# Two-layer block with experts and state space: ACT's small slots, an earlier sum of outputs, the second experts' table and stores in pieces

## What is computed

```python
h = _layernorm(x) * (1 + ca) + sa
x = x + ga * _L0_attn_ref(h, ...)      # causal attention, 16 heads of 8, rotary
h = _layernorm(x) * (1 + cb) + sb
x = x + gb * _L0_ffn_ref(h, ...)       # 8 experts, top 2 by softmax, a shared expert
h = _layernorm(x) * (1 + ca) + sa      # vectors of the second layer from here on
x = x + ga * _L1_attn_ref(h, ...)      # state space
h = _layernorm(x) * (1 + cb) + sb
x = x + gb * _L1_ffn_ref(h, ...)       # 8 experts of width 352, top 2 by score
```

```python
x_in = x @ in_W.T + in_b
K = jnp.exp(dtA[:, :, None] * jnp.arange(Lseq))
k = 2.0 * jnp.einsum('hn,hnl->hl', Ceff, K).real
y = irfft(rfft(u, n=2 * Lseq) * rfft(k, n=2 * Lseq))[..., :Lseq] + u * D_skip[:, None]
y = gelu(y)
a, g = split(glu_W @ y + glu_b)
out = (a * sigmoid(g)) @ out_W.T + out_b + x
```

## Time and profile before

| what | value |
|---|---|
| three timed runs | 1283.17, 1283.76, 1278.12 us (median 1283.17) |
| profiled execution | 1280.39 us, span 1279.1 us |
| mean granted clock of TensorE | 0.86 of full speed |
| busy share of the span | PE 75%, DVE 66%, ACT 54%, PE's weight loads 49%, POOL 35% |
| front, until its barrier opens | 130.3 us |
| attention, projection, routing and experts of layer 0 | until 865.9 us |
| state space, its gate | until 977.3, until 1010.0 us |
| routing, experts, last sum of layer 1 | to about 1082, 1240, 1279 us |

### The profile page before, as it was taken

The page is one execution under the profiler, slowest core; times in us unless marked ns, Lnnn a source line. Parts: engine busy times, 40 slices in busy tenths (PEclk is TensorE's granted clock), DMA queues, the critical chain, the costliest instruction groups (busy, mean ns, idle before and its releaser), DMA issues. The chain is left out here.

```text
span 1279.1 us, 26922 instructions
## 1 busy us (share of the span) xinstructions
PE 955.5 (75%) x9014; PEld 621.1 (49%) x9014; DVE 848.6 (66%) x2087; ACT 689.3 (54%) x1475; POOL 443.8 (35%) x510
## 2 busy tenths in 40 slices
PE   4554589899998998987477979961756656898990
PEld 2232233333333333324355568861645445898990
DVE  6765788888888888824765336646776786543435
ACT  3684067777777777774334447752602223565660
POOL 5636012322321122210375327760000066674440
PEclk9777589999999999989577989995868855998995
DMA  8125002111111100000211123328553332232216
GB/s 205 66 101 207 29 8 79 42 35 35 50 48 39 35 27 26 2 1 1 64 61 58 38 66 95 96 65 260 136 134 101 101 92 78 70 85 78 64 54 203
DMA packets 116286, 97.16 MB, mean 76 GB/s; under 512 B 15437, under 2 KB 102568, under 8 KB 116152
## 3 DMA queue, kind: packets, MB, share of 16 engines
q1 hardware_dynamic: 101976, 75.30, 20.4%
q0 software_dynamic: 8704, 17.97, 4.1%
q10 hardware_dynamic: 5472, 2.17, 0.6%
HBM read 60.18 MB, written 34.95 MB: 74 GB/s over the span
## 5 line engine op out<-in xcount | busy, mean ns | idle before, releaser
L844 DVE TENSOR_REDUCE part<-sps 128x2 f32<-128x1024 f32 (+2 forms) x320 | 341.6, 1114 | 65.1 <-PE sps L725 43.0
L819 ACT ACTIVATE prob<-tpa 128x1024 f32<-128x1024 f32 (+1 forms) x208 | 193.0, 928 | 77.5 <-PE tpa L761 74.5
L655 POOL TENSOR_SCALAR_AFFINE_SELECT prob<-prob 128x512 f32<-128x512 f32 x128 | 79.7, 634 | 357.0 <-ACT prob L819 357.0
L1578 POOL DMA_INDIRECT yk<-yo,place x144 | 146.8, 1019 | 129.9 <-ACT yo L1607 107.0
L819 ACT ACTIVATE prob<-tpb 128x512 f32<-128x512 f32 (+1 forms) x224 | 128.4, 573 | 63.5 <-PE tpb L761 63.5
L781 PE MATMUL ops<-prob,vs 128*32 128x512 f32 (+3 forms) x1536 | 160.3, 505 | 1.5 <-POOL prob L655 1.5
L718 PE MATMUL sps<-qk 48*128 48x512 bf16 (+3 forms) x768 | 135.6, 344 | 31.7 <-DVE part L844 21.7
L1186 POOL DMA_INDIRECT xg<-h,slot x128 | 124.7, 975 | 84.0 <-DVE slot L1309 46.8
L1691 PE MATMUL banks<-xT,y 128*128 128x128 f32 x864 | 111.3, 280 | 5.1 <-issue 3.5
L1633 DVE COPY place<-xt 128x1 uint32<-128x1 uint32 x144 | 22.0, 153 | 135.9 <-ACT esg L1601 93.4
L1691 PEld LDWEIGHTS banks<-xT,y 128*128 128x128 f32 x864 | 105.4, 197 | 5.6 <-issue 5.6
(11 more groups left out here) (337 smaller groups left out, 1835.1 us busy)
## 6 DMA issues: line engine op xcount, KB each, us to landing
xt<-xg SPq DMA_DIRECT2D x144, 65.0 KB
qk<-term SPq DMA_DIRECT2D x24, 256.0 KB, 2.7
qk<-qk SPq DMA_DIRECT2D x64, 96.0 KB
arena<-kpad SPq DMA_DIRECT2D x6, 1024.0 KB, 11.8
powers<-powr SPq DMA_DIRECT2D x8, 516.0 KB, 5.3
powr<-powers SPq DMA_DIRECT2D x4, 1032.0 KB, 8.8
qk<-qk SPq DMA_DIRECT2D x64, 64.0 KB
arena<-yk SPq DMA_DIRECT2D x16, 256.0 KB, 5.7
```

Source lines behind the costliest of these rows:

```text
L655: nc.gpsimd.affine_select(out=blk, in_=blk, pattern=[[0, HQ], [1, P]], compare_op=ALU.is_ge, fill=0.0, base=0, channel_multiplier=-1).then ...
L819: nc.scalar.activation(prob[:, at:at + len(units), 0:n], slot_of(t, m)[:, :, 0:n], ACT.Exp, scale=float(HD) ** -0.5).then_inc(exp_done, 1)
L844: freed(nc.vector.tensor_reduce(to, src, AX.X, ALU.max, negate=True))
L1578: nc.gpsimd.indirect_dma_start(out=d.yk, out_offset=bass.IndirectOffsetOnAxis(ap=place[:, u:u + 1], axis=0), in_=yo[u][:], in_offset=None) ...
```

## The change

It has three parts, and some small moves that go with them.

**In the front**, ACT's state space work is cut into smaller slots. `scalar(act, s)` becomes `scalar(act, s, place)`: place 0 stands between `high` and `middle`, place 1 at the step's end. The magnitudes spread over steps 2 to 5 and the sines over steps 5 to 8, one group a place (the magnitudes one or two). The kernel sums start in step 7 instead of 5. DVE's coefficients move from its fifth step to its seventh (s == 6). The waits for the landing of the kernels and powers move out of the front into SP's part of the attention; for this the tile `powr` and both semaphores live in the scope around both.

**The first sum** (`first_sum`) begins in the first layer's program. SP issues all 16 gathers of `yk` there, behind the landing of all results, into `w.v` and `w.y`, and DVE does `combine(0)`, `combine(1)` and the first batch's statistics there. In `s4_core` the other parts are summed in another order around the shifts (`AHEAD`, `BEHIND`), and ACT's `norm(b)` also waits for part b + 4. SP loads there the powers first and then the first four kernel matrices without a wait. The output bias is added to `h` in four pieces between copies of states, the passes over h and x at the end are gone, and the residual of the gate phase has three operations: product + h, x gate, + x.

**In the second layer** the sets of weights stand one batch earlier where they can, so that none is left behind the last batch's ranks. The last wave's table is made in four pieces, one a tile at n = 4 to 7. The eight stores of empty rows stand one each behind the loads of tiles 24 to 31, and their landing is waited for ahead of tile 40. The first layer keeps its tables and tails.

```diff
+                    s4.scalar(act, s, 0)
+                    if s > 0:
                         middle(s - 1)
...
-                    s4.scalar(act, s)
+                    s4.scalar(act, s, 1)
...
                     if s == 4:
                         gates()
+                    if s == 6:
                         s4.coefficients(dve)
...
-    SINES = {3: (0, 1), 4: (2, 3), 5: (4, 5), 6: (6, 7)}
-    SUMS = {5: (0, 1), 6: (2, 3), 7: (4, 5), 8: (6, 7)}
+    MAGNITUDES = {(2, 1): (0,), (3, 0): (1, 2), (3, 1): (3,), (4, 0): (4, 5), (4, 1): (6,), (5, 0): (7,)}
+    SINES = {(5, 1): (0,), (6, 0): (1,), (6, 1): (2,), (7, 0): (3,), (7, 1): (4,), (8, 0): (5,), (8, 1): (6, 7)}
+    SUMS = {7: (0, 1, 2), 8: (3, 4, 5, 6, 7)}
+    KERNELS = {(8, 0): (0, 1), (8, 1): (2, 3, 4, 5, 6, 7)}
...
-        sp.wait_ge(p_kept, 16 * NI)
-        sp.wait_ge(k_kept, 16 * (1 + GI))
...
+                    if t == 0:
+
+                        sp.wait_ge(w.k_kept, 16 * (1 + GI))
                     if t < len(rows_of):
...
                 sp.wait_ge(rows_in, 16 * (len(rows_of) - 1))
+                sp.wait_ge(w.p_kept, 16 * (NG // GI))
```

```diff
+                if layer == 0:
+                    sp.wait_ge(experts.sh_added, NB)
+                    for s in range(2 * NB):
+                        w.first.load(sp, s)
+                else:
                     combined.sync(sp)
...
+                if layer == 0:
+                    w.first.combine(dve, 0)
+                    w.first.combine(dve, 1)
+                    w.first.statistics(dve, 0)
+                else:
                     combined.vector(dve)
...
+                AHEAD, BEHIND = ([2], [5], [6], []), ([3, 4], [], [7], [])
                 for b in range(NB):
+                    for s in AHEAD[b]:
+                        combine(dve, s)
+                    shifts(b)
+                    for s in BEHIND[b]:
+                        combine(dve, s)
                     if b + 1 < NB:
-                        combine(2 * b + 2)
-                    shifts(b)
-                    if b + 1 < NB:
-                        combine(2 * b + 3)
-                        statistics(b + 1)
+                        statistics(dve, b + 1)
...
+                    if n % 2 == 1:
+
+                        hb = h[:, n // 2 * TPB:(n // 2 + 1) * TPB, :]
+                        v.tensor_tensor(hb, hb, m.outb[:].rearrange("p (o c) -> p o c", o=1).to_broadcast([P, TPB, C]), ALU.add)
...
                     act.wait_ge(shifted, b + 1)
+                    act.wait_ge(x_done, b + 5)
...
-                    link(v.tensor_tensor(o[u][:], po[:, u, :].rearrange("p (j c) -> p j c", j=4),
-                                         w.gate[:, 2, bass.ds(b, 1), :].to_broadcast([P, 4, C]), ALU.mult))
+                    hs = m.h_keep[:, b * TPB + u * 4:b * TPB + u * 4 + 4, :]
+                    v.tensor_tensor(o[u][:], po[:, u, :].rearrange("p (j c) -> p j c", j=4), hs, ALU.add).then_inc(o_read, 1)
+                    dve.wait_ge(o_read, s + 1)
+                    link(v.tensor_tensor(o[u][:], o[u][:], w.gate[:, 2, bass.ds(b, 1), :].to_broadcast([P, 4, C]), ALU.mult))
```

```diff
+    else:
+        WEIGHTS_AT = [([0, 1], [2]), ([3, 4], [5]), ([6], [7]), ([], [])]
...
-            if layer == 1 and n == 4:
-                routed.tables(dve, len(waves) - 1)
+            if layer == 1 and 4 <= n < 8:
+
+                next(table)
...
             sp.dma_start(xt[n % UN][:], rows[bass.ds(at, 1)][0]).then_inc(x_in[n % UN], 16)
+            if layer == 1 and waves[0][1] <= n < waves[0][1] + NE:
+                routed.tail(sp, n - waves[0][1])
```

136 lines of the change are left out of this document (71 added, 65 removed).

## The result

| | before | changed |
|---|---|---|
| median of four executions each | 1281.82 us | 1249.76 us |
| all four | 1278.12 to 1283.76 | 1245.36 to 1254.02 |
| span of the profiled execution | 1279.1 us | 1244.0 us |

The ratio is 0.9734, with a 95% interval of 0.9704 to 0.9764: 2.7% faster, 32 us. I had forecast 1257 with a range of 1247 to 1268, a gain of 26 against the median then known. The sum was 6 us short of that.

The account below looks back on a forecast made before the run. PE bounds the second experts' stretch; elsewhere whoever reaches the closing barrier last. Terms -6.5, -6.0, +1.1, -3.6, -3.8, -6.6 sum to -25.4, taking 1280.4 to 1255.0 us; forecast 1257 (the profiled execution lay below the median), range 1247 to 1268.

Parts of the forecast that it names:

- Front, -6.5: Front: 2.4 us from the landing, 2 from POOL's chain, 2.1 from SP's queue, together 6.5 us gained.
- the coefficients' 3.8: Front, DVE: the coefficients take 3.8 us and, moved behind the seventh step, end at 91.6, so POOL starts 4.7 later.
- The estimate of 2.9: Front, POOL: by SBUF contention the last four groups cost 2.9 us each, ending the front about 1 us earlier; not summed.
- they run from 119.3 to 123.9: Front, SP: the last four kernel stores, with nothing left ahead of them, start at 119.3 and end at 123.9 us.
- Way into the state space, -6.0: First layer's end: gathers fill SP's idle time, barrier 5.8 us later, first row operation 10.0 behind it, 6.0 gained.
- rival C: Gathers at the first layer's end crowd each other at 1.0 us each: barrier 874.7, gain 2.7, kernel 1260.3; chance 0.07.
- Gate, +1.1: State space gate: a third operation a step costs 1.85 us, fewer semaphores to clear give 0.75 back, 1.1 lost.
- the 14 us of passes: State space's end: removing DVE's three big passes gains nothing, since they ended within 0.1 us of the last store's landing.
- Second layer, -14.0: Second layer's program: earlier weight sets 3.6 us, table in pieces 3.8, stores of empty rows one by one 6.6, all gained.
- All 3.8 go: Second layer's experts: the table in four pieces fits DVE's idle time, removing the whole 3.8 us pause, at the least 3.
- Rival D: Second layer's experts: POOL's scatters replace the removed pauses, the 6.6 us return as waits, kernel 1264; chance 0.08.
- Rival E: Second layer's experts: without the pauses PE gets tiles at half clock, each 2.12 us more, kernel slower or even; chance 0.05.

Follow-up runs that it names:

- c_coef5: Changed kernel with DVE's coefficients one step earlier, on its sixth step (s == 5) instead of the seventh: 1252.27 us, ratio 0.9758 to the kernel before.
- u_slots: Changed kernel with ACT's front slots, coefficients and kernel sums back in their old places, landing still awaited in the attention: 1260.88 us, ratio 0.9838 to the kernel before.
- u_sum: Changed kernel with all 16 gathers, two combinations and first statistics back behind the first layer's barrier, new sum order kept: 1265.77 us, ratio 0.9855 to the kernel before.
- u_gate: Changed kernel with the three output passes back at the state space's end and two gate operations a step: 1365.25 us, against 1370.0 for the changed kernel on the same chip.

## Why the prediction was right, and where it fell short

**Front, -6.5, was -9.3 (-9.8 by the mean of the fronts).** DVE's seventh step ended at 88.4, as forecast (88), but by luck. DVE's waits for the first cast up to there fell by 13.4 (19.9 to 6.5), not by 17; and the coefficients' 3.8, which had stood ahead of this step and now stand behind it, I had not taken off. The two errors cancel. The steps on POOL hold: start at 91.6 forecast, 92.2 measured; end 117.5, measured 117.2; last kernel out of ACT 119.3, measured 119.0. I had priced the last four groups at 3.1, and they took 2.82; the first four took 3.4 each, where I had used 3.65, which is the mean of all eight and not of those beside a busy DVE. The estimate of 2.9 that I had set beside the sum, by the contention that the Trainium skill describes (SBUF — State Buffer, "Who interferes with whom"), was the nearer one. The trace agrees with the page: no pair was above 2.52 once DVE had stopped, each of the two pairs of 3.50 had beside it one DVE operation with two inputs from SBUF (at 99.37 and 103.01), and 3.1 of the 4.5 us by which c_coef5 lengthened the chain fell beside a busy DVE. The term that was mis-sized is "they run from 119.3 to 123.9": the stores took 1.58, not 4.57. I had taken the duration of an issue as its own, though I had just removed what stood ahead of it in the queue. u_slots brought back 4.69 together with the late stores of q and k, and in six profiles the stores' time went roughly with the DMA share just ahead of them. The landing was 2.4, as said.

**Way into the state space, -6.0, was -7.7.** Barrier 5.8 later forecast; 4.8 in this pair of profiles, 4.1 to 5.8 over the others. By the mean of the seven profiles named at u_sum (262.5 and 100.4) the part gives 5.8, so the forecast was closer than the pair shows: the changed kernel's profile in the pair is 1.9 below the mean in these two programs. Sixteen gathers took 12.6, forecast 12.9; rival C (1.0 each) did not happen. From the skill's limit (DMA: Bandwidth & Descriptors, "Where 436 GB/s comes from") they would have taken 11.7; 4.2 MB in 12.6 us are 333 GB/s, and the first eight, 2.1 MB in 5.45, came to 385 GB/s at their issue, above the page's 358. But that is the rate of issue, not of the data: from 844 to 860 the DMA engines, busy all the time (share 1.02), moved 263 GB/s, below the page's limit. The 10.0 from the barrier to the first row operation were exact. Rival C's own number is off by a little: a barrier at 874.7 and 10.0 behind it leave 2.9, not 2.7. What the step didn't see is that SP would hold the barrier by only 1.5 us over DVE.

**Gate, +1.1, was +0.8,** within what the stage varies: 33.0 to 34.2 in the profiles of the changed gate, 32.7 twice in the kernel before. SP's first load comes 2.35 behind the barrier instead of 3.00, near the 0.75 forecast. What the third operation costs stays open: between DVE's first and last operation 1.3 us more than before in this pair, not 1.85, but only 0.2 more than in u_gate, which takes it away again. That the 14 us of passes gain nothing was right: in u_gate they end 2.4 ahead of the barrier.

**Second layer, -14.0, was -13.5,** and the parts were 3.5, 3.0 and 6.3 by the programs' lengths, 3.3, 2.8 and 5.9 by PE's rows, against 3.6, 3.8 and 6.6. The mis-sized term is the table: "All 3.8 go" is not so, since PE's lead over DVE doesn't take the longer pieces. The five tiles from the first piece on lose 0.95, and 3.8 - 0.95 is the 2.8 measured. Rival D did not come: PE waits 0.2 us in the whole stretch, for nothing of POOL's, and is busy 139.76 of 140.00. Rival E was wrong in its direction: without the pauses the clock stayed at full. One number of mine was a slip: "a stretch of the second experts near 144" doesn't follow from my own terms, which give 158 - 10.4 = 147.6. Measured alike it was 9.4 shorter, 148.6. Another slip is the upper end of the range: "with the same spread" D's 1264 reaches 1272, not 1268.

**What was not in the sum** are the attention's 4.4 us and the projection's 1.0, by which the profiled pair differs. They are PE's granted clock in these executions; whether a part of them comes from the change isn't shown. Without them the pair is 29.7 apart; the sum said 25.4, and the 4.3 between are the front's 2.8, the way into the state space with 1.7 and the gate's 0.3, less 0.5 in the second layer. The 1.7 are luck of this pair, as its two programs lie 1.9 below their mean. So by the means of the profiles the touched stages give some 28 of the medians' 32.1, and the last 4 us stay open: the attention varies by 10, and both of its pairs favour the changed kernel by 4.

## What to carry to other kernels

The duration of a DMA's issue in a row belongs to what stands ahead of it in the queue as much as to itself: when an edit empties the queue, reprice the issues behind it (4.6 us became 1.6 here). Where an engine waits at a barrier for another engine's drain, work of the next program that needs only finished data fits there, up to the point where the next engine in line holds the barrier; read all the drains, not only the last. A chain on POOL is shorter beside an idle DVE, so starting it earlier gains less than the head start (7.3 us gave 2.8). And a gain at one operation isn't yet one of the program: the gathers split five and three brought the first row operation 1.2 us forward, and the end of the stage 0.1 to 0.2.

## What the runs showed of the hardware

POOL's drain at the end of a layer's program took 10.5 to 11.4 us in every profile. Its record starts ahead of the last two scatters (854.4, with the last scatter from 856.21 to 857.17 in the kernel before) and ends 8.5 to 8.6 us behind the last one. In the kernel before and in u_sum it held the first layer's barrier 7 us beyond SP; with the gathers ahead of the barrier SP or DVE comes later.

The kernel before took 1281.8 us in the first group of runs, 1285.5 and 1289.3 in the next two, and 1394.8 in the last (these three on chips 0, 9 and 5). Whether the chip or the time of the run makes the difference isn't shown. Of the 113 us between its two profiles 107 lie in the two layers' programs (59.3 and 47.6) and 5.6 in the attention. The first layer's program in both:

```profile
608.60:865.90 257.30, 196.06 (x1237) 159.91 (x1237) 139.63 (x623) 132.22 (x407) 142.14 (x146) 0.84 0.24 68
614.50:931.10 316.60, 208.65 (x1237) 163.57 (x1237) 140.18 (x623) 131.20 (x407) 141.80 (x146) 0.84 0.19 55
```

The first layer's program took 257.30 in the first profile and 316.60 on that chip; front, state space, gate and projection agree to 0.3. The engines' busy times rise by 13 us on PE, by 4 on its weight loads and change by at most 1 on the others, so most of it is waiting. The lists of waits of the two layers' programs there have entries that the first profile doesn't have, whose releaser the trace can't name. One of them:

```profile
ACT sg L1379 <- remote: 37.1, 5, 9.6
```

What these engines waited for isn't shown, and I leave it open. The change gives 24.8 us in that group by the medians, where it gave 32.1 in the first group, and the intervals of the two ratios (0.9781 to 0.9868 and 0.9704 to 0.9764) do not meet. The profiled pair on that chip is 30.9 apart, and of its stages the first layer's program differs most from the first pair (+8.8 instead of +4.8; the others by at most 1.2). The layers' programs vary there by several us from one kernel to the next (first layer 323.8 to 327.6, second 299.9 to 307.2 in three profiles of kernels that are nearly alike), so where the missing 7 us are is open too.
